# The sum of drive and bias moved from VectorE in PSUM to GpSimd in SBUF, and other slots for an FFN's work

## The reference, cut to what matters

```python
def derivative(q, p, drive, coupling, bias):
    dq = q - q**3/3 - p + drive + tanh(q) @ coupling.T + bias
    dp = EPSILON * (q + ALPHA - BETA*p)
# per time step: four derivatives (Runge-Kutta 4), each at a state made from the one before,
# then q_next, p_next, both clipped to +-20; q_next is the step's output
# FFN on the outputs: per-row absolute maximum -> scale -> fp8 rounding -> gate and up products
# -> silu(gate) * up -> per-row maximum -> fp8 rounding -> down product -> plus x1
```

## Time and profile before

| | us |
|---|---|
| median of 3 runs | 1735.76 (1735.63 to 1736.38) |
| profiled execution, device time | 1733.82 |
| its span, first to last instruction | 1732.0 |
| stages of the integration (first to last L1317) | 1079.8 to 1686.1 |
| tail behind them | 45.9 |

### The profile page before, as it was taken

How to read it: one execution, slowest core, us unless ns; L and a number is a source line. 1 busy time by engine, 2 the same in 40 slices (tenths; PEclk the granted TensorE clock), 3 DMA queues, 4 the chain that set the end, 5 groups by cost and what they waited for, 6 DMA issues and landing times.

```text
span 1732.0 us, 45724 instructions
## 1 busy us (share of the span) xinstructions
PE 1551.0 (90%) x16744; PEld 951.5 (55%) x16744; DVE 1126.0 (65%) x3319; ACT 507.8 (29%) x1589; POOL 380.3 (22%) x554
## 2 busy tenths in 40 slices
PE   5999899999859999999999998788888888888884
PEld 2333333333738576675767753556666666666662
DVE  2888743333786475664747541568888888888885
ACT  1233211112120202102020110355555555555552
POOL 1222010000000000000000000235555555555554
PEclk9999999999969999999999998999999999999997
DMA  7322210005000000000000005101111111111111
GB/s 303 79 76 61 79 29 12 12 11 111 1 0 1 25 0 24 6 18 23 1 24 0 24 6 184 42 23 29 33 31 44 35 35 33 30 33 30 42 35 35
DMA packets 88432, 70.27 MB, mean 41 GB/s; under 512 B 30728, under 2 KB 80824, under 8 KB 87352
## 3 DMA queue, kind: packets, MB, share of 16 engines
q1 hardware_dynamic: 86616, 63.75, 12.7%
q0 software_dynamic: 1760, 5.77, 1.2%
HBM read 52.55 MB, written 16.92 MB: 40 GB/s over the span
## 4 chain that ended last, share of the span: by engine, by line
PE 69%; DVE 14%; issue 8%; ACT 5%; DMA 2%; POOL 1%; SPq 1%; ACTq 0%; DVEq 0%; POOLq 0%
PE ps L681 13%; PE ps L671 13%; PE ps L775 10%; PE ps L588 9%; PE ps L596 9%; PE ps L715 3%; PE ps L765 2%; PE ps L739 2%; ACT mem L964 2%; DVE mem L1317 2%; DVE mem L1275 2%; ACT ps L956 2%; PE ps L692 1%; PE ps L789 1%; PE ps L585 1%
## 5 line engine op out<-in xcount | busy, mean ns | idle before, releaser
L775 PE MATMUL ps<-mem 128*32 128x128 f32 x8192 | 280.7, 278 | 89.7 <-ACT mem L964 85.6
L775 PEld LDWEIGHTS ps<-mem 128*32 128x32 f32 x8192 | 212.8, 111 | 165.2 <-ACT mem L964 118.3
L671 PE MATMUL ps<-mem 128*128 128x512 f32 x512 | 224.6, 593 | 0.0
L681 PE MATMUL ps<-mem 128*128 128x256 f32 x1024 | 222.3, 379 | 0.0
L681 PEld LDWEIGHTS ps<-mem 128*128 128x128 f32 x1024 | 194.2, 190 | 25.8
L514 POOL TENSOR_TENSOR mem<-mem 128x128 f32<-128x128 f32 x64 | 30.7, 480 | 784.7 <-ACT mem L959 784.5
L588 PE MATMUL ps<-mem 128*32 128x384 f32 x2048 | 181.5, 496 | 0.0
L596 PE MATMUL ps<-mem 128*32 128x384 f32 x2048 | 179.0, 491 | 2.7 <-DVE mem L1122 2.7
L671 PEld LDWEIGHTS ps<-mem 128*128 128x128 f32 x512 | 95.7, 190 | 109.6 <-issue 109.2
L518 POOL TENSOR_TENSOR mem<-mem 128x128 f32<-128x128 f32 x192 | 101.2, 527 | 171.8 <-ACT mem L959 165.7
L765 PE MATMUL ps<-mem 128*128 128x128 f32 x768 | 138.6, 304 | 0.0
(11 more groups left out here) (129 smaller groups left out, 2104.8 us busy)
## 6 DMA issues: line engine op xcount, KB each, us to landing
mem<-x_scr SPq DMA_DIRECT2D x128, 64.0 KB, 1.8
mem<-in_xT SPq DMA_DIRECT2D x64, 64.0 KB, 1.8
mem<-in_Wq SPq DMA_DIRECT2D x1, 4096.0 KB
mem<-in_Wo SPq DMA_DIRECT2D x1, 4096.0 KB
mem<-in_x SPq DMA_DIRECT2D x16, 256.0 KB, 2.7
x_scr<-mem SPq DMA_DIRECT2D x32, 128.0 KB, 2.3
q_scr<-mem SPq DMA_DIRECT2D x64, 64.0 KB, 1.6
mem<-q_scr SPq DMA_DIRECT2D x64, 64.0 KB, 1.9
```

Of the source, the lines that this page charges most:

```text
L671: mm = pe.matmul(ps[:, 6 + pr, :], aoT[:, h, pr * P:pr * P + P], wo[:, h, :], start=(h == 0), stop=(h == HEADS - 1))
L681: mm = pe.matmul(ps[:, h % Q_BANKS, 0:BLK], wq[:, c, h * DH:(h + 1) * DH], xnb[:, c, :], start=(c == 0), stop=(c == NC - 1))
L775: mm = pe.matmul(ps[32 * j:32 * j + 32, st % 2, 0:P], thT[:, c, :], ct[:, c, j * P:(j + 1) * P], start=False, stop=(c == NC - 1), skip_gro ...
```

## The change

The sum of drive and bias becomes a POOL instruction in slots 0, 4, 8 and 12, written to a double-buffered SBUF tile `dsum` for the next time step; the seeds read `dsum` in place of the PSUM tile, so that both operands of a seed lie in SBUF. The FFN's work is laid into other slots: silu (ACT) from 12, 13, 0, 2 to 13, 14, 1, 3; t_kept (ACT, L992) from 1, 4 to 0, 5; the input's scaling (ACT, L1002) from 6 to 4, its maximum and scale (DVE) from 5 and 6 to 3; the gated row's maximum is taken in four pieces of 352 columns in slots 1, 2, 5, 6 in place of two of 704 in slots 3 and 6, and its scale in slot 6 in place of 7. A copy of one column keeps the scale's old value until slot 8. The order of PE's work and POOL's own slots stay, and two waits of ACT ahead of the groups go.

```diff
+        dsum = [f32(w.take(P), P) for _ in range(2)]
@@ POOL
+            def drive_sum(t, s, loads):
+                pool.wait_ge(drive_ld[s], 16 * loads)
+                wait_if(pool, rk_seed, 4 * t - 4)
+                pool.tensor_tensor(dsum[s % 2], drive[s], biasq, ALU.add).then_inc(rk_drive, 1)
@@ POOL, group
                     if rk:
                         p_step(4 * g + k // 4, k // 4, k % 4)
+                        if k % 4 == 0 and not (isinstance(g, int) and g == NTILE - 1 and k == 12):
+                            drive_sum(4 * g + k // 4 + 1, (k // 4 + 1) % 4, g + 1 + (k == 12))
                     slot(k, tile)
+            pool.wait_ge(rk_start, 3)
+            drive_sum(0, 0, 1)
@@ ACT, slot
-                    if k == 6:
+                    if k == 4:
                         act.wait_ge(f_rq, i + 1)
-                    if k in (12, 13):
-                        silu_part(i, k - 12)
+                    if k in (13, 14):
+                        silu_part(i, k - 13)
-                    if k in (0, 2):
+                    if k in (1, 3):
                         silu_part(i, 2 + k // 2)
-                    if k == 1:
+                    if k == 0:
                         t_kept(i, 0)
-                    if k == 4:
+                    if k == 5:
                         t_kept(i, 1)
-            act.wait_ge(ct_ld, 16 * 4)
-            act.wait_ge(rk_bits, 1)
@@ DVE
-                dve.tensor_tensor(driven(s), drive[s], biasq, ALU.add).then_inc(rk_drive, 1)
-                    dve.tensor_tensor(o, driven(s), p, ALU.subtract).then_inc(rk_seed, 1)
+                    dve.tensor_tensor(o, dsum[s % 2], p, ALU.subtract).then_inc(rk_seed, 1)
-                    dve.scalar_tensor_tensor(out=o, in0=p, scalar=float(SEEDS[st][0]), in1=driven(s), op0=ALU.mult, op1=ALU.add).then_inc(rk_seed, 1)
+                    dve.scalar_tensor_tensor(out=o, in0=p, scalar=float(SEEDS[st][0]), in1=dsum[s % 2], op0=ALU.mult, op1=ALU.add).then_inc(rk_seed, 1)
-                if st == 2 and not end:
-                    drive_sum(t + 1, (s + 1) % 4, g + 1 + (s == 3))
@@ DVE, slot
-                    if k == 5:
+                    if k == 3:
                         dve.wait_ge(q_ld, 16 * TILE_T * (i + 1))
-                        v.did(dve.tensor_reduce(xam, qt, AX.X, ALU.max, apply_absolute_value=True))
-                    if k == 6:
-                        v.need(v.n)
-                        if tile(1) is not None:
-                            dve.wait_ge(f_gated, GU_T * tile(1) + GU_T)
-                        v.need(v.did(dve.tensor_scalar(xsx, xam, 1.0 / FP8_MAX, None, ALU.mult)))
-                        dve.reciprocal(xrs, xsx).then_inc(f_rq, 1)
+                        v.need(v.did(dve.tensor_reduce(xam, qt, AX.X, ALU.max, apply_absolute_value=True)))
+                        v.need(v.did(dve.tensor_scalar(xnew, xam, 1.0 / FP8_MAX, None, ALU.mult)))
+                        dve.reciprocal(xrs, xnew).then_inc(f_rq, 1)
+                    if k == 8:
+                        if tile(1) is not None:
+                            dve.wait_ge(f_gated, GU_T * tile(1) + GU_T)
+                        v.did(dve.tensor_copy(xsx, xnew))
-                    if k in (3, 6):
-                        half = k // 6
-                        dve.wait_ge(f_gated, GU_T * i + 2 * half + 2)
-                        v.did(dve.tensor_reduce(tam2[:, half:half + 1], tt[:, half * 2 * GU_N:(half + 1) * 2 * GU_N], AX.X, ALU.max,
-                                                apply_absolute_value=True))
-                    if k == 7:
+                    if k in (1, 2, 5, 6):
+                        m = (1, 2, 5, 6).index(k)
+                        dve.wait_ge(f_gated, GU_T * i + m + 1)
+                        v.did(dve.tensor_reduce(tam4[:, m:m + 1], tt[:, m * GU_N:(m + 1) * GU_N], AX.X, ALU.max, apply_absolute_value=True))
+                    if k == 6:
                         v.need(v.n)
-                        v.need(v.did(dve.tensor_reduce(tam, tam2, AX.X, ALU.max)))
+                        v.need(v.did(dve.tensor_reduce(tam, tam4, AX.X, ALU.max)))
```

More of the change, by code:

```diff
@@ L85 @@
 T_PARTS = ((0, 6 * P), (6 * P, INNER))
-GROUP_STEPS = 12
+GROUP_STEPS = 15
 def wait_if(eng, sem, value):
@@ L264, in gru_attn_rk4_ffn @@
         yout = f32(w.take(D), D)
-        tam2 = f32(w.take(2), 2)
-        tam, tsx, tsy, trs, xam, xsx, xrs = (f32(w.take(1), 1) for _ in range(7))
+        tam4 = f32(w.take(4), 4)
+        tam, tsx, tsy, trs, xam, xnew, xsx, xrs = (f32(w.take(1), 1) for _ in range(8))
         (wih_ld, whh_ld, w_att, b_ld, c_ld, xt_ld0, xt_ld1, h0_ld, st_ld, wg_ld, wu_ld, idx_ld, wd_ld, x_ld, x1_wr, q_ld, x1_ld,
@@ L1293, in seed @@
                     wait_if(dve, rk_p, t)
-                    dve.tensor_tensor(o, driven(s), p, ALU.subtract).then_inc(rk_seed, 1)
+                    dve.tensor_tensor(o, dsum[s % 2], p, ALU.subtract).then_inc(rk_seed, 1)
                 else:
-                    dve.scalar_tensor_tensor(out=o, in0=p, scalar=float(SEEDS[st][0]), in1=driven(s), op0=ALU.mult, op1=ALU.add).then_inc(rk_seed, 1)
-            drive_sum(0, 0, 1)
+                    dve.scalar_tensor_tensor(out=o, in0=p, scalar=float(SEEDS[st][0]), in1=dsum[s % 2], op0=ALU.mult, op1=ALU.add).then_inc(rk_seed, 1)
             seed(0, 0, 0)
@@ L1351, in slot @@
                         dve.tensor_scalar(eq, eq, FP8_TINY, ROUND_AT, ALU.max, ALU.mult).then_inc(f_xe, 1)
+                    if k == 8:
+                        if tile(1) is not None:
+                            dve.wait_ge(f_gated, GU_T * tile(1) + GU_T)
+                        v.did(dve.tensor_copy(xsx, xnew))
                     if k in (12, 13):
+                        if k == 12:
+                            v.need(v.n)
                         gate_part(i, k - 12)
```

## The result

The changed kernel takes 1806.4 us (median of 4 runs, 1803.8 to 1809.6), 4.1% more than before: the ratio to before is 1.0409, with an interval of 1.0391 to 1.0427. The forecast was 1778.5 with a range of 1756 to 1807, so the direction and the kind of loss were as forecast, and the size lies at the range's far end, on the time of the first rival (1806). The profiled execution took 1803.8 us, its span is 1802.0.

A forecast was written before the change was run, and what follows sets the result against it. The chain between state updates was taken as the bound, with seeds newly waiting for POOL. Some 2.8 us a steady group, twelve times 33.8, plus edge groups and tail gave +42.8 on 1733.8; 1778.5 us forecast as median, range 1756 to 1807.

The forecast's parts named there:

- the first rival: Slot 12: POOL starts first, the first seed waits, then the second; some +2.1 us more a group, 1806 us; chance 0.14.
- What bounds the kernel: Every stage: the chain between state updates, 2.12 us in a plain slot; slot 8 takes 3.53, with L1395 held up by POOL.
- The wait belongs to two SBUF operands: All 256 seeds: DVE instructions with both operands in SBUF wait for POOL; a blocked seed ends 0.16 us behind POOL's end.
- Rival 2: All seeds: not held up by POOL, leaving a gain of 1.5 us a group, 1715 us; chance 0.06.
- Slot 0: First seed waits for POOL's L536 and the work queued behind it is late: +1.25 us a group.
- slot 4: First seed waits for POOL's L529 and ends at 1392.10 for 1391.63: +0.47 us a group.
- silu: Slots 1 and 13: moved a slot later, silu no longer delays square and tanh; 0.15 us gained each, twice a group.
- Slot 8: First seed waits for L543, second for L548 behind the new sum, L1395 shortens to some 0.56 us: +0.80 us net.
- Slot 12: First seed taken as unblocked despite L563's 0.02 us lead, L563 0.16 longer, second seed later: +0.25 us a group.
- slot 13: Its seed waits for L536, which the new sum delays to end at about 1415.15 for 1414.36: +0.35 us a group.
- The granted clock: PE's longer idle stretches lower the granted clock for a while, to 1790 us or more; chance 0.04.
- group 1: Only slot 8's POOL pair L543 and L548 is present; the slot grows to about 3.8 us: +1.6 us.

The follow-up runs named there:

- pool_extra: Kernel before plus one POOL tensor_tensor of 128 columns in slots 0, 4, 8 and 12, its result unread: 1724.1 us, ratio 0.9936.
- slots_only: Changed kernel with its new FFN slots, but the sum of drive and bias given back to DVE in PSUM: 1716.0 us, ratio 0.9887.
- sbuf_operands: Kernel before with one edit: DVE still makes the sum, but into SBUF, so seeds have two SBUF operands: 1792.9 us, ratio 1.0343.
- probe: Separate kernel copying input to output, sweeping starts of 208 POOL/DVE instruction pairs; two-SBUF-operand forms take 1.2 to 1.39 us when POOL leads 23 to 130 ns.
- seed_first_12: Changed kernel plus a POOL wait in slot 11, so the final FFN sum starts after the next step's first seed: 1776.5 us, ratio 1.0244.

## Why the prediction was right, and where it failed

*What bounds the kernel.* Right: the chain from one state update to the next, with slot 8 held by L1395 behind POOL. pool_extra and slots_only each free that instruction. In pool_extra slot 8 falls by 1.03 us and a group, at best, by 1.00; in slots_only slot 8 falls by 1.17 and a group by 1.51, where silu gives most of the rest.

*The wait belongs to two SBUF operands.* Right, read from two pairs of rows and shown by sbuf_operands, where only the operand's place changes, and by probe. Rival 2 (seeds not held up, 1715) fell; the 1716.0 of slots_only is what that rival would have given, by leaving the operands in PSUM.

*Slot 0, slot 4, silu.* +1.24 for +1.25, +0.48 for +0.47, -0.19 for -0.15 twice: right to a few hundredths.

*Slot 8.* The mechanism was right, and the term too large: +0.53 for +0.80. I had put L548 at about 2.42 us behind the state update, by 0.58 for the new sum and gaps of 0.07; in the changed kernel L555, the same instruction, starts 2.18 behind it (1389.68, with the update at 1387.50), since POOL's instructions followed each other with no gap on the record and the sum took 0.50:

```profile
1389.21 0.50 POOL L531 TENSOR_TENSOR mem<-mem 128x128 f32<-128x128 f32 x1
...
1389.68 1.28 POOL L555 TENSOR_TENSOR mem<-mem 128x512 bf16<-128x512 f32 x1
...
1390.16 0.96 DVE L1296 SCALAR_TENSOR_TENSOR ps<-mem 128x128 f32<-128x128 f32 x1
```

*Slot 12* is the step that failed: "The pair L518/L1285 with the same 0.02 went to DVE, and both starts follow the same release (L524), so I take the seed as unblocked and L563 as 0.16 longer". The first seed took 1.39 us for 0.30, the second 1.49 for 0.28, and the slot grew by 2.31 us and not 0.25. The two leads were nearly the same, 22 ns and 24, and the state of POOL was not; the row's bracket said that POOL had been idle there, and in slot 12 it had not. I took one pair as the rule for another without asking in what they differ. In place of the wait that the forecast had put into slot 13 (+0.35) there was none, as the first rival had it. The first rival had the place and the price: I gave +2.1 a group over the forecast, and seed_first_12 gives 42.33 - 40.67 = 1.66 at full clock; the rest of its 30 us is clock and the groups at the edges. That 1806.4 meets the rival's 1806, to which I gave 0.14, is partly luck: its group would be 38.05 + 2.8 + 2.1 = 42.95 us for the measured 42.33, 7 us too much over twelve groups, and the half clock, at nothing in that sum too, brought 11.8. Of the Trainium skill's rule for the shared ports (SBUF — State Buffer, § Who interferes with whom), that the first to start has them for the whole instruction, the forecast had said that one row speaks against it. The changed kernel sides with the rule, and the other runs with a reserve: where POOL led by over 26 ns by the record, DVE's instruction of two SBUF operands waited in every pair of the eleven traces, and below that the recorded order doesn't settle it.

*The granted clock.* I had given 0.04 to a fall of the clock and nothing to its price in the sum. It fell in the changed kernel and in its relatives: TensorE is at 2.4 GHz throughout groups 3 to 15 of the kernel before, and in the changed kernel the spells at 1.2 GHz begin at 1175.3, 1216.3, 1229.9, 1274.3, 1359.6, 1445.0, 1574.7 and 1704.4 us. Of the changed kernel, around the sixth (columns as in the earlier trace rows):

```profile
1442.00:1444.97 2.97, 1.08 (x32) 0.82 (x32) 2.62 (x5) 0.91 (x4) 2.94 (x3) 1.00 0.05 15
1444.97:1451.80 6.83, 6.06 (x46) 3.78 (x46) 3.90 (x13) 2.74 (x11) 3.08 (x6) 0.50 0.34 90
```

PE was busy 1.08 of the 2.97 us ahead of the fall, while both seeds waited. The twelve groups 3 to 14 take 519.8 us, 12 x 42.33 would be 508.0: the half clock costs 11.8 us. That the waits make it fall is what seed_first_12 and slots_only suggest, with three fewer spells and with one. The same waits stand in each of the twelve groups, though, and the clock fell in six of them; no run changed the clock alone, so this is argued and not shown.

*The other terms.* First to last state update 675.8 us for 606.3, so +69.5: groups 3 to 14 +63.2 (12 x 4.28 and the 11.8), groups 0, 1, 2 and 15 together +6.3, for which I had 7.8. That hides an error in group 1: -0.2 for +1.6, since its slot 8 grew by only 1.0 and the kernel before had a spell at half clock there, at 1118.1 us, that the changed one has not. The tail behind them takes 47.1 us for 45.9, +1.2 for +0.8. The lead-in shows no loss: the first state update is at 1079.1 us for 1079.8, within what the parts that were not touched vary by, so the +0.4 can't be told.

## What to carry to other kernels

Whether a VectorE instruction has one operand in PSUM or both in SBUF can matter more than its length: before moving an operand from PSUM to SBUF to relieve an engine, list which GpSimd instructions run beside each reader, and add up their remaining lengths. In a chain of short steps one should look at who is in front at each meeting, and a meeting decided by some ten nanoseconds has to be carried in the range at both prices, or be ordered by a wait. And a change of two parts is worth taking apart: here one half gained 1.1%, and was hidden by the other's 5%.

## What the runs showed of the hardware that I had not expected

Who wins when a GpSimd instruction starts just ahead of a VectorE instruction with two SBUF operands turns within nanoseconds. In the probes, over 120 pairs, it is between 22 and 23 ns of POOL's recorded lead if POOL was idle and between 15 and 16 if it came from an instruction of its own (for tensor_tensor the nearest pairs are 22 and 24, and 14 and 18); in pool_extra between 9 and 16 behind an instruction of its own; and in sbuf_operands an idle POOL still lost at 26. The price is uneven. A losing POOL is longer by at most 0.16 us behind 128 columns of DVE, and by 0.37 behind the 768 of slots_only; a losing seed waits for the end of whatever POOL runs, up to 1.2 us more in the changed kernel and up to 1.6 in sbuf_operands (1.89 us). And a GpSimd instruction that nobody needs made the kernel before 0.6% faster, by keeping another one back.
